# Two attention stages of a twelve-stage kernel: one PSUM bank per score product, 64-row score matmuls and masks, scores first in each slot, bf16 bias rows, and the setup moved inside the rounds

## What is computed

```python
# first attention ("rotary"), 16 heads of 8 channels, over all 512 keys
qkv = x @ w_qkv + b_qkv
q = apply_rope(q); k = apply_rope(k)
w = softmax(einsum('bhqd,bhkd->bhqk', q, k / sqrt(8)))
out = einsum('bhqk,bhkd->bhqd', w, v) @ w_out + b_out

# third attention ("alibi"), 16 heads of 8 channels, causal, no biases
scores = einsum('bhqd,bhkd->bhqk', q, k) / sqrt(8) - slope_h * (key - query)
scores = where(key <= query, scores, -inf)
out = einsum('bhqk,bhkd->bhqd', softmax(scores), v) @ Wo.T
```

## Time and profile before

| what | value |
|---|---|
| median of the runs (3 runs, 6522.61 to 6527.36) | 6523.39 us |
| the profiled execution: its time | 6504.49 us |
| the profiled execution: its span | 6502.7 us |
| mean granted clock of TensorE | 0.839 of 2.4 GHz |
| busy: TensorE, VectorE, ScalarE, GpSimd | 73%, 64%, 36%, 27% |
| rotary attention, from its first load to its last first score | 130.3 to 1268.0 us |
| alibi attention, likewise | 3837.5 to 4727.8 us |

### The profile page before, as it was taken

The page is one execution under the profiler, slowest core; times in us unless marked ns, Lnnn a source line. Parts: engine busy times, 40 slices in busy tenths (PEclk is TensorE's granted clock), DMA queues, the critical chain, the costliest instruction groups (busy, mean ns, idle before and its releaser), DMA issues. The chain is left out here.

```text
span 6502.7 us, 116141 instructions
## 1 busy us (share of the span) xinstructions
PE 4777.8 (73%) x40092; PEld 2867.1 (44%) x40313; DVE 4184.9 (64%) x9235; ACT 2331.6 (36%) x4415; POOL 1750.0 (27%) x2105
## 2 busy tenths in 40 slices
PE   3699999967673066476576647999966599977998
PEld 2233333333342055444333434444434377755776
DVE  7566666568897811288798965555569655476554
ACT  2365556630142010344101114555531144422444
POOL 2443343210143300033103433433324311054110
PEclk8899999988886555766687769999987699988999
DMA  1212112000033142510000002222200000000000
GB/s 38 46 37 42 32 39 40 17 5 0 16 119 104 32 116 66 112 39 29 9 0 0 0 16 48 51 49 49 43 1 0 18 1 0 1 1 1 1 0 26
DMA packets 230199, 202.44 MB, mean 31 GB/s; under 512 B 23553, under 2 KB 203867, under 8 KB 229339
## 3 DMA queue, kind: packets, MB, share of 16 engines
q1 hardware_dynamic: 229787, 196.88, 12.8%
HBM read 118.68 MB, written 72.88 MB: 29 GB/s over the span
## 5 line engine op out<-in xcount | busy, mean ns | idle before, releaser
L542 DVE TENSOR_REDUCE rotary_maxima<-rotary_ps_s 128x2 f32<-128x1024 f32 x512 | 616.9, 1221 | 414.5 <-PE rotary_ps_s L716 412.9
L765 ACT ACTIVATE rotary_probs<-rotary_ps_s 128x512 f32<-128x512 f32 x1024 | 556.1, 596 | 386.1 <-PE rotary_ps_s L732 371.3
L542 DVE TENSOR_REDUCE alibi_maxima<-alibi_ps_s 128x2 f32<-128x256 f32 (+3 forms) x512 | 412.8, 822 | 372.3 <-PE alibi_ps_s L719 368.9
L2052 DVE SCALAR_TENSOR_TENSOR x<-moe_ps_out,moe_weights,x 128x128 f32 (+1 forms) x1024 | 285.7, 344 | 457.7 <-PE moe_ps_out L2093 429.9
L2093 PEld LDWEIGHTS moe_ps_out<-w_moe_w,moe_hidden 128*128 128x128 f32 x4096 | 495.0, 192 | 108.3 <-issue 80.7
L765 ACT ACTIVATE alibi_probs<-alibi_ps_s 128x512 f32<-128x512 f32 (+3 forms) x1024 | 402.6, 440 | 339.6 <-PE alibi_ps_s L735 334.6
L2093 PE MATMUL moe_ps_out<-w_moe_w,moe_hidden 128*128 128x128 f32 x4096 | 500.6, 275 | 0.0
L2080 PE MATMUL moe_ps_hidden<-moe_z,w_moe_w 128*128 128x512 f32 x1024 | 488.4, 599 | 0.0
L2142 ACT ACTIVATE moe_hidden<-moe_ps_hidden,w_moe_b 128x512 f32<-128x512 f32 x512 | 345.8, 688 | 359.6 <-PE moe_ps_hidden L2080 348.0
L932 PE MATMUL moe_ps_experts<-w_moe_w,moe_normedT 128*128 128x512 f32 x512 | 307.7, 754 | 124.8 <-DVE moe_others L900 124.8
L732 PE MATMUL rotary_ps_s<-rotary_q_stack,rotary_k_stack 128*128 128x512 bf16 x1017 | 339.3, 392 | 30.7 <-ACT rotary_probs L765 7.3
(11 more groups left out here) (457 smaller groups left out, 10543.7 us busy)
## 6 DMA issues: line engine op xcount, KB each, us to landing
rotary_parts<-rotary_part SPq DMA_DIRECT2D x96, 128.0 KB, 2.2
rotary_q_stack<-rotary_parts SPq DMA_DIRECT2D x192, 64.0 KB
rotary_k_stack<-rotary_parts SPq DMA_DIRECT2D x192, 64.0 KB
convolve_bands<-in_filters SPq DMA_DIRECT2D x192, 64.0 KB, 2.7
alibi_parts<-alibi_part SPq DMA_DIRECT2D x96, 128.0 KB, 2.2
alibi_q_stack<-alibi_parts SPq DMA_DIRECT2D x192, 64.0 KB
alibi_k_stack<-alibi_parts SPq DMA_DIRECT2D x192, 64.0 KB
delta_n<-convolved SPq DMA_DIRECT2D x16, 256.0 KB, 2.0
```

The lines of the kernel that those rows point to most:

```text
L542: v.tensor_reduce(maxima[:, blk, 2 * pair:2 * pair + 2], ps_s1[t % 2][:, :, 0:keys_of(blk)], AXIS.X, ALU.max).then_inc(s.max_made, 1)
L765: nc.scalar.activation(probs[u % 8][:, 0:T - lo], ps_s2[m][:, 0:T - lo], ACT.Exp).then_inc(s.exp_made, 1)
L2052: v.scalar_tensor_tensor(xb, ps_out[e % 2][:, b:b + 1, :], weights[par][:, b, e:e + 1], xb, ALU.mult, ALU.add).then_inc(s.added, 1)
```

## The change

- PSUM: three single banks for the first scores and three for the second (was two double and two single). The two heads of a slot use banks u % 3 and (u + 1) % 3 with u = 2t, shifted by the round.
- VectorE takes one maximum for each head: 64 reduces over one bank in a round, where there were 32 over two banks.
- The q stack has one slab for each pair of heads, as the k stack has. The score matmuls take rows 0 to 63 for one head and rows 64 to 127 for the other. The mask matmuls of alibi are 64 rows too: two parts for each head, of which the second uses copies of the mask tensors with the two halves of rows swapped (six DMAs in the setup).
- Order in a TensorE slot: first scores, second scores, `pv`, and then the work in `bank`; its slots are moved (norm transpose and projections from 4, 6, 8, 10, 12 to 1, 3, 5, 9, 11; v from 17 to 19; last quad 2 to 7; maxima 19 to 17; a quad 29 to 27; output products stay in 23 and 13).
- The bias of v and of the output product in rotary: one bf16 matmul of three rows over all 512 columns instead of four f32 ones of one row; the rows are cut once by `BiasRows.cut`.
- Setup: statistics and normalisation of sequence 0 come first on VectorE, which fills only the first q stack; ScalarE fills the first k stack, and the other stacks at the end of rounds 0 and 1. `dve_normalise` of the next sequence stands in slot 31 instead of slot 1 of its round, `dve_statistics` in 16 instead of 28.
- The loop is gone: all 19 rounds are written out.

```diff
-def rounds(eng, seqs, run, at_loop=lambda r: None):
...
+def rounds(eng, seqs, run):
+    for r in range(seqs + 3):
         run(r, r % 3)
...
-    PROJECTS = (4, 6, 8, 10, 12, 17) if rope else (4, 6, 8, 17)
+    PROJECTS = (1, 3, 5, 9, 11, 19) if rope else (1, 3, 5, 19)
-    QUADS = (15, 21, 29)
+    QUADS = (15, 21, 27)
+    LAST_QUAD, OT_SLOT, MAXIMA_SLOT, OUT_SLOT = 7, 13, 17, 23
...
-    qs = [ph.sb(f"q_stack{j}", [P, HEADS, T], BF16) for j in range(3)]
+    qs = [ph.sb(f"q_stack{j}", [P, PAIRS, T], BF16) for j in range(3)]
-    ps_s1 = [ph.ps(f"s1_{j}", [P, 2, T]) for j in range(2)]
-    ps_s2 = [ph.ps(f"s2_{j}", [P, T]) for j in range(2)]
+    ps_s1 = [ph.ps(f"s1_{j}", [P, T]) for j in range(3)]
+    ps_s2 = [ph.ps(f"s2_{j}", [P, T]) for j in range(3)]
...
-                        v.tensor_reduce(maxima[:, blk, 2 * pair:2 * pair + 2], ps_s1[t % 2][:, :, 0:keys_of(blk)],
-                                        AXIS.X, ALU.max).then_inc(s.max_made, 1)
+                        for two in range(2):
+                            u = 2 * t + two
+                            dve.wait_ge(s.s1_done, 64 * b + u + 1)
+                            v.tensor_reduce(maxima[:, blk, 2 * pair + two:2 * pair + two + 1], ps_s1[(j - 1 + u) % 3][:, 0:keys_of(blk)],
+                                            AXIS.X, ALU.max).then_inc(s.max_made, 1)
...
+            dve.wait_ge(s.stack_loaded, 16 * CONSTANTS)
+            v.tensor_copy(qs[0][:], q_rows[:].unsqueeze(2).broadcast_to([P, PAIRS, T])).then_inc(s.q_set, 1)
+            norm.dve_normalise(dve, 0, 0)
...
+                        mm(bank[:], k.ones3[:], bias.rows[:, 0:C].unsqueeze(1).broadcast_to([3, BLK, C]), start=True, stop=False)
                     for b in range(BLK):
-                        last = mm(blocks(b), nT[:, b * P:(b + 1) * P], w.wv, start=True, stop=not rope)
-                        if rope:
-                            last = mm(blocks(b), k.ones_row[:], w.rows[:, 0:C], start=False, stop=True)
+                        last = mm(blocks(b), nT[:, b * P:(b + 1) * P], w.wv, start=not rope, stop=not rope or b == BLK - 1)
...
+                        for two in range(2):
+                            u = 2 * t + two
+                            rows = slice(two * ROWS, (two + 1) * ROWS)
+                            at_least(pe, s.max_made, 64 * b + u - 2)
+                            last = mm(ps_s1[(jb + u) % 3][:, 0:n], qs[jb][rows, pair, blk * P:(blk + 1) * P],
+                                      ks[jb][rows, pair, 0:n], start=True, stop=not causal)
...
+                            for part in range(2):
+                                for two in range(2):
+                                    rows = slice(two * ROWS, (two + 1) * ROWS)
+                                    last = mm(ps_s1[(jb + 2 * t + two) % 3][:, n - P:n], masks[part][0][rows, :], masks[part][1][rows, :],
+                                              start=False, stop=part == 1)
...
+                            at_least(pe, s.exp_made, 64 * c + u - 2)
+                            last = mm(ps_s2[(jc + u) % 3][:, 0:T - lo], ks[jc][rows, pair, kb * P:(kb + 1) * P], qs[jc][rows, pair, lo:T],
+                                      start=True, stop=not causal)
...
-                            at_least(pe, s.exp_made, 64 * c + u - 1)
-                            last = mm(ps_s2[m][:, 0:T - lo], ks[jc][:, h // 2, kb * P:(kb + 1) * P], qs[jc][:, h, lo:T],
-                                      start=True, stop=not causal)
...
+                if isinstance(r, int) and r < 2:
+                    fill(qs[r + 1], q_rows[:].unsqueeze(2))
+                    fill(ks[r + 1], probs[7][:].unsqueeze(1))
```

178 lines of the change are left out of this document (93 added, 85 removed).

## The result

The kernel after takes 6102.14 us (median of 4 runs, 6092.66 to 6109.03) where the kernel before takes 6523.0 us (median of 4, 6512.15 to 6527.36): ratio 0.9356, 95% interval 0.9338 to 0.9374, 421 us less. The forecast was 6105 us.

The account below looks back on a forecast made before the run. No single engine but a TensorE-ScalarE chain was taken as the bound. Rotary -277 and alibi -142 us took the profiled 6504.5 to 6085, plus 18.9: 6105 us; own range 6040 to 6200, 8 in 10 6020 to 6330.

Parts of the forecast that it names:

- The chain of 3.32 us: Two rotary slots before: exponentials 1.12, wait 0.35, `pv` 0.99, scores to next exponentials 0.86 us; forecast 2.83 after.
- the third bank: Second scores go out earlier, leaving a hand-over of some 0.07 us instead of 0.35 between last exponential and `pv`.
- The pair of scores: Two 64-row matmuls in different array halves and banks: 0.22 us together, bounds 0.215 (overlap) and 0.43 (none).
- The rotary round: Full rotary round: 45.3 us of chain plus bank work, VectorE additions and round end makes 51.1, taken as 52 us.
- The alibi round: Full alibi round: 6.7 us off for halves and banks, 0.9 for order, from 51.85 to about 44.3 us.
- The changes of tile shape: TensorE, each visit to `bank`: 0.10 us into `pv` plus 0.14 out taken as price, 0.24 us added.
- The setup: Start of each attention: 24 us saved in rotary, 21 in alibi; moved fills can delay round 2 by some 4 us.
- The sum: Rotary stage -277 us, alibi stage -142, together -419; profiled execution 6085 us, plus 18.9 for the median: 6105 us.
- Halves that do not overlap: Rival: score pairs run one after the other, rotary rounds about 60 us, alibi 55, total 6380 us; chance 0.12.
- The k stack came in time: Rival was a late k stack: its loads land too late for the next round, 56 us rounds, 6165 us; chance 0.09.
- The clock: Rival: 64-row matmuls run at 1.2 GHz like small tiles, every matmul doubles, 7075 us; chance 0.04.
- VectorE sets the pace: Rival: four reduces take 3.0 us against 2.83, about 3 us a round, 6150 us; inside the forecast's range, no own chance.

Follow-up runs that it names:

- The ladder: Stage-length steps from before to after with 128-row scores and two banks per product, then third banks restored, then row halves: 195, 118 and 102 us.
- masks128: Kernel after with each alibi mask as one 128-row matmul per head instead of two 64-row ones, scores still 64 rows: 6179.1 us, ratio 0.9474.
- setup_first: Kernel after with all memsets and the six stack fills on VectorE ahead of the first normalisation, no ScalarE fills in rounds 0 and 1: 6124.6 us.
- full_rows: Kernel after with 128-row scores and masks again and a zero-padded q slab for each head: 6199.0 us, ratio 0.9507.
- one_half: Kernel after with all score and mask matmuls in rows 0 to 63, same instruction form and count, odd heads wrong: 7832.7 us, ratio 1.2015.
- two_banks_s2: Kernel after with two banks instead of three for the second scores, first scores keeping three: 6174.2 us, ratio 0.9468.
- f32_bias: Kernel after with the biases of v and output product as four f32 one-row matmuls each instead of one bf16 matmul: 6171.6 us, ratio 0.9474.
- before_unrolled: Kernel before with its rounds written out instead of looped, nothing else: 6491.4 us, ratio 0.9966.

## Why the prediction was right

**What bounds the kernel.** The chain of 3.32 us stood, and undoing its parts brings its parts back: the third bank 0.32 us in a plain pair (forecast 0.28), the halves 0.22 (3.00 against 2.78; forecast 3.05 against 2.83).

**The pair of scores.** Forecast 0.22 us with 0.02 between the two; measured 0.22 with 0.01. The share that the prediction took from the 3.07 times of the Trainium skill (TensorE: Matmul & The Clock Gate, Part 3) for four 32-row tiles would have had 0.28. It does not carry over: this trace has two tiles of 64 rows overlap in full.

**The rotary round.** Forecast 51.1, taken as 52; measured 49.76. The sixteen intervals from `pv` to `pv` (374.42 to 424.18 us) add up as 16 x 2.78 = 44.5, + 1.5 for four projections (forecast 0.8), + 1.5 for v and out (2.5), 0 for the quads (0.6), + 1.2 for statistics and the maxima in slot 17 (0.9), + 1.15 at the round's end (1.0) = 49.8. The terms missed in both directions by up to 1 us and the forecast of 51.1 was 1.3 us too high; the 0.9 us for small waits did not exist in plain rounds. The largest miss is v and the output product: the forecast had 2.1 us for v, by 0.42 us for each f32 matmul, and the trace has 1.41.

**The alibi round.** Forecast 44.3, measured 44.86 in plain rounds and 45.0 on average. Of the 7.6 us that the forecast takes off a round, 6.7 were for the halves and the banks, and 0.9 for the order. The ladder has the shares otherwise: 51.85 to 49.32 us before either (2.5), to 46.42 with the third banks (2.9) and to 44.86 with the halves (1.6). So halves and banks were worth 4.5 us and not 6.7, and the order and what comes with it 2.5 and not 0.9. The two errors go against each other.

**The changes of tile shape.** From a score pair to the transposes 0.09 us (382.28 less 381.97 + 0.22) and back 0.17 (382.87 - 382.28, less 0.42 for four transposes); between 64 and 128 rows in bf16 0.1 each way (masks128). The forecast had 0.24 for both. The rule of the Trainium skill (TensorEngine Tiling (Array Packing), Key Properties), that a change of mode drains the array, agrees with the 0.1 us each way of masks128; twice the price is not seen.

**The setup.** First load to first transpose: 137.03 - 130.60 = 6.4 us instead of 30.9, 24.5 less (forecast 24), and in alibi 9.2 instead of 30.9, 21.7 less (forecast 21). The fills hold up round 2 by 7 us in rotary, where the forecast had 4. So setup_first shows a net worth of 14.3 + 5.8 = 20 us where 24 + 21 less 4 was forecast: its start is 20.5 us later in each attention, but it gets back 2.8 and 6.9 us in rounds 0 and 2 of rotary and 5.1, 5.8 and 3.6 us in rounds 0 to 2 of alibi, into which the kernel after has moved VectorE's memsets (round 0) and the fills. Those of round 1 are within what this round differs by from kernel to kernel.

**The sum.** Rotary stage -293.0 us (forecast -277), alibi -122.6 (forecast -142), other stages +16. So the total is as close as it is by luck, through misses that offset each other. Rotary was forecast 16 us too little: its twelve rounds take 20.6 us less than 12 x 52. Alibi was forecast 19 too much, with 9 us in its twelve rounds (540.3 instead of 531.6) and some in round 1, on which the forecast had put nothing: it took 49.1 us before and takes 54.9, at a clock of 0.51, and the runs do not divide that between the clock and the moved work. The 18.9 us that the forecast put on the profiled time were not there: the profiled run of the kernel after took 6105.3, its median is 6102.1. The forecast of 6085 for that execution was 20 us too low, of which 16 are the other stages, and that addition covered it.

**The rivals.** *Halves that do not overlap* did not happen. full_rows, which makes the pair as slow, has rounds of 56.8 and 46.4 us where the rival had 60 and 55: it over-counted work that lies in free time, and in alibi it had twice as many masks. *The k stack came in time*: no round waits for it after round 0. But the same paragraph of the prediction had the rows of the maximum behind it in the queue with thin cover, and these do come late, in four of twelve rotary rounds and two alibi rounds of the kernel after, and these six rounds take 9.4 us more in all than plain ones. The forecast had a price for this path only at a late k stack. *The clock* was nearer than its chance of 0.04 looked: round 1, with 64-row pairs and projections but no `pv`, runs at 0.50 (53.8 us) and full_rows' at 0.84 in the same 35 us, and one_half stays at 0.50 throughout. In the kernel after three of the 24 full rounds dip to 0.96 or 0.97, 2 us each, and each fall starts within 0.8 us after a wait for the rows of the maximum; rounds with such a wait of 1.1 and 1.3 us have none, so the wait alone does not bring it. *VectorE sets the pace* holds for 1.9 of 49.8 us.

## What to carry to other kernels

In a queue that runs in order, put work that nobody waits for behind the work that starves others: here undoing that alone cost 171 us, where the whole change brings 421, and no instruction is more or less by it. A third buffer pays only in the stretches where the engine behind it has time left, so count those, not all. When rounds get shorter, look again at every path through DRAM whose result the next round needs: here no full round waits for the rows of the maximum at 51.9 us a round (two_banks_s2), and some do at 49.8. Two matmuls in the two row halves of the array run at the same time only if their rows differ, and if one half stands empty the clock goes with it; look at the granted clock whenever a matmul's rows shrink.

## What the runs showed of the hardware

- Half-filled arrays keep the clock down: with all scores in rows 0 to 63 the granted clock is 0.50 (1.2 GHz) in rounds in which TensorE is busy 108.8 of 109 us. The same instructions in both halves run at 1.00.
- Even both halves do not hold it in all mixtures. In round 1, before the first `pv`, the 64-row pairs run at 0.50, with 128-row scores at 0.84 in the same stretch (185 to 220 us).
- One-row f32 matmuls in turns with 128-row ones are followed by a fall to 1.2 GHz: in nine of twelve rounds with 64-row pairs (f32_bias, 1.4 to 2.9 us each), and in six and seven of twelve with 128-row scores (before and before_unrolled, 1.2 us). With one three-row bf16 matmul in their place no full rotary round has a fall there. A back edge of a hardware loop also comes with 0.94 or 0.95 in its round. What exactly makes the clock fall is not settled by these runs.
- An f32 matmul of 128 columns occupies 0.27 us in a row of four of one shape, and 0.42 when 128-row and one-row ones take turns (1.09 us for four in the kernel after, 3.33 for eight in f32_bias).
- Code that was not touched took from 2480.9 to 2507.1 us in fourteen kernels. Why is open; a difference of some 10 us between totals should be looked for in the stages first.
